# Second expert layer of a mixture block: hidden values computed transposed, from weights copied per tile

## What is computed

```python
shared = jax.nn.silu(xf @ Sg) * (xf @ Su) @ Sd
probs = jax.nn.softmax(xf @ Wr, axis=-1)
topk_p, topk_i = jax.lax.top_k(probs, K)
cw = jnp.zeros((T, n_exp), x.dtype).at[jnp.arange(T)[:, None], topk_i].add(topk_p)
def step(acc, ew):
    wg, wu, wd, c = ew
    y = jax.nn.silu(xf @ wg) * (xf @ wu) @ wd
    return (acc + y * c[:, None], None)
```

## Time and profile before

| | |
|---|---|
| median of 3 runs | 1652.86 us (1652.83 to 1653.16) |
| profiled execution: its own time | 1644.97 us |
| profiled execution: span, mean granted TensorE clock | 1643.2 us, 0.956 |
| busy in the span: TensorE passes, weight loads | 1487.4 us (91%), 1114.3 us (68%) |
| busy: VectorE, ScalarE, GpSimd | 1018.6 us (62%), 736.6 us (45%), 572.3 us (35%) |
| second expert stage, first transpose of x to last scatter | from 1444.9 us to 1584.4 us of the span |

### The profile page before, as it was taken

The page is one execution under the profiler, slowest core; times in us unless marked ns, Lnnn a source line. Parts: engine busy times, 40 slices in busy tenths (PEclk is TensorE's granted clock), DMA queues, the critical chain, the costliest instruction groups (busy, mean ns, idle before and its releaser), DMA issues. The chain is left out here.

```text
span 1643.2 us, 31228 instructions
## 1 busy us (share of the span) xinstructions
PE 1487.4 (91%) x9905; PEld 1114.3 (68%) x9905; DVE 1018.6 (62%) x3468; ACT 736.6 (45%) x1544; POOL 572.3 (35%) x994
## 2 busy tenths in 40 slices
PE   5999999983999999699799999999999597589987
PEld 3776676772999999565566666666666386468876
DVE  3345555453444444499898888888886286645558
ACT  3444444430222222345177777777777242244420
POOL 4123333344222222245532332322333165635530
PEclk9999999986999999899899999999999798889999
DMA  7001111115777777668857666667761575745556
GB/s 234 1 26 36 49 46 52 39 58 157 212 212 213 212 212 212 211 229 259 203 75 98 98 90 90 92 89 98 98 89 40 143 240 187 171 129 156 161 159 220
DMA packets 150592, 221.74 MB, mean 135 GB/s; under 512 B 23648, under 2 KB 98144, under 8 KB 150304
## 3 DMA queue, kind: packets, MB, share of 16 engines
q1 hardware_dynamic: 127904, 170.58, 45.2%
q0 software_dynamic: 13344, 36.55, 6.4%
q10 hardware_dynamic: 9184, 12.61, 2.5%
HBM read 141.16 MB, written 78.25 MB: 134 GB/s over the span
## 5 line engine op out<-in xcount | busy, mean ns | idle before, releaser
L2095 ACT ACTIVATE t_probs<-t_ps_st 128x512 f32<-128x512 f32 x576 | 313.2, 597 | 124.9 <-PE t_ps_st L2147 122.4
L2073 DVE CUSTOM_DVE_ANT_0 whole_sum<-t_ps_s,t_later 128x512 bf16<-128x512 f32 (+3 forms) x512 | 285.5, 586 | 14.0 <-PE t_ps_s L2133 11.9
L2049 POOL TENSOR_SCALAR_AFFINE_SELECT t_probs<-t_probs 128x128 f32<-128x128 f32 x512 | 137.4, 300 | 330.5 <-ACT t_probs L2095 328.9
L2133 PE MATMUL t_ps_s<-t_ks,t_qs 96*128 96x512 f32 (+3 forms) x768 | 247.8, 362 | 0.5 <-ACT t_neg_max L2085 0.5
L2147 PE MATMUL t_ps_st<-t_qs,t_ks 128*128 128x512 f32 (+3 forms) x768 | 242.7, 365 | 0.8 <-ACT t_probs L2095 0.8
L2147 PEld LDWEIGHTS t_ps_st<-t_qs,t_ks 128*128 128x128 f32 x768 | 136.8, 189 | 73.6 <-ACT t_probs L2095 40.2
L2073 DVE CUSTOM_DVE_ANT_0 whole_sum<-t_ps_s,t_later,t_first_max 128x512 bf16<-128x512 f32 (+3 forms) x256 | 140.5, 549 | 47.8 <-PE t_ps_s L2133 47.8
L2162 PE MATMUL t_ps_o<-t_probs,t_vs 128*17 128x256 f32 (+1 forms) x2560 | 154.9, 361 | 0.5 <-ACT whole_sum L2102 0.5
L2133 PEld LDWEIGHTS t_ps_s<-t_ks,t_qs 96*128 96x128 f32 x768 | 138.7, 190 | 18.0 <-DVE t_first_max L2073 1.6
L1460 POOL DMA_INDIRECT outputs_dram<-m_y,m_place x71 | 68.1, 959 | 208.8 <-DVE m_place L1535 201.1
L1490 PE MATMUL m_ps_h<-m_xt,m_w_t 128*128 128x128 f32 x1136 | 140.7, 278 | 0.0
(11 more groups left out here) (340 smaller groups left out, 2652.1 us busy)
## 6 DMA issues: line engine op xcount, KB each, us to landing
m_w_t<-in_w_dram SPq DMA_DIRECT2D x71, 512.0 KB, 4.4
t_qs<-qkt_dram SPq DMA_DIRECT2D x128, 128.0 KB, 5.6
t_ks<-qkt_dram SPq DMA_DIRECT2D x128, 128.0 KB, 5.7
m_x_t<-gathered_dram SPq DMA_DIRECT2D x79, 128.5 KB, 2.1
m_x_t<-gathered_dram SPq DMA_DIRECT2D x71, 129.0 KB, 2.1
d_ye<-outputs_dram SPq DMA_DIRECT2D x8, 1024.0 KB, 8.2
qkt_dram<-d_hi ACTq DMA_DIRECT2D x32, 256.0 KB, 5.2
qkt_dram<-d_lo SPq DMA_DIRECT2D x32, 256.0 KB, 7.2
```

The source lines that it names most:

```text
L2049: nc.gpsimd.affine_select(out=diag, in_=diag, compare_op=ALU.is_ge, fill=0.0, base=0, pattern=[[1, P]], channel_multiplier=-1).then_inc(ma ...
L2073: nc.vector.tensor_tensor_reduce(out=seen[:, (NP * p + x) % (RS + 1), 0:keys], in0=bank_of(p, x)[:, 0:keys], in1=masks, scale=1.0, scalar= ...
L2095: nc.scalar.activation(probs[:, p % 2, i // NST, base:base + STC], ps_st[(NX * p + i) % RT][:], ACT.Exp, scale=HD ** -0.5).then_inc(exp_re ...
L2133: nc.tensor.matmul(bank_of(p, x)[:, 0:keys], q[0:MAX_ROW, head, qc * P:(qc + 1) * P], k[0:MAX_ROW, head, k0:k0 + keys], start=True, stop=T ...
```

## The change

`run_experts` is removed and `run_gated_experts` takes its place for the second expert stage. ScalarE copies the gate and up weights of a tile's expert (128 partitions x 512 elements) from `wgu_sb` to a ring of three (`m_w_t`), two tiles ahead. The first layer takes them as stationary operand in blocks of 128 and streams x^T of 128 columns: four float32 products in place of two, and `m_ps_h` has hidden channels on its partitions. The products of the gate are therefore h^T already, so `turn_h`, `m_ps_ht` and its copy are gone, and VectorE writes `m_ht` itself. The loop is a turn shorter, the second layer stands two tiles behind the transposes of x in place of three, `m_ps_x` has two buffers, and ScalarE looks up experts too. SyncE's and GpSimd's programs are unchanged.

```diff
-def run_experts(nc, sb, pb, sem, c, name, E, gathered, outputs, kept, up, down, weights, late, by_row=False):
...
+def run_gated_experts(nc, sb, pb, sem, c, E, gathered, outputs, kept, w_up, w_down, weights, late):
+    ident = c["ident"]
+    n_list = 2 * NT + E - 1
+    F1 = P
+    tiles = kept["tiles"]
+    x_t = sb("m1_x_t", [P, RING, DM + 1])
+    w_t = sb("m1_w_t", [P, 3, KD, 2 * F1])
+    xt = sb("m1_xt", [P, 2, KD, P])
+    sig = sb("m1_sig", [P, 2, P])
+    act_g = sb("m1_act_g", [P, 2, P])
+    ht = sb("m1_ht", [P, 2, P])
+    y = sb("m1_y", [P, RING, DM])
+    place, spare = sb("m1_place", [P, n_list], U32), sb("m1_spare", [P, n_list])
+    ps_x = [pb(f"m1_ps_x{s}", [P, 2 * DM]) for s in range(2)]
+    ps_h = [pb(f"m1_ps_h{s}", [P, 4, P]) for s in range(2)]
+    ps_y = [pb(f"m1_ps_y{s}", [P, 2 * DM]) for s in range(2)]
+    x_loaded = [sem(f"m1_x_loaded{s}") for s in range(RING)]
+    stored = [sem(f"m1_stored{s}") for s in range(RING)]
+    place_taken, spare_ready, w_ready = sem("m1_place_taken"), sem("m1_spare_ready"), sem("m1_w_ready")
+    xt_done, xt_ready, h_done, sig_ready, gated, h_ready, y_done, y_ready = (sem("m1_" + n) for n in (
+        "xt_done", "xt_ready", "h_done", "sig_ready", "gated", "h_ready", "y_done", "y_ready"))
+
...
+    with nc.Block(no_gpsimd_drain=True) as block:
...
+        @block.tensor
+        def _(pe):
+            expert = {}
+
...
+            def turn_x(t):
+                pe.wait_ge(x_loaded[t % RING], 16 * (t // RING) + 16)
+                wait(pe, xt_ready, t - 1)
+                for j in range(KD):
+                    last = nc.tensor.transpose(ps_x[t % 2][:, j * P:(j + 1) * P], x_t[:, t % RING, j * P:(j + 1) * P], ident[:])
+                last.then_inc(xt_done, 1)
+
+            def go_up(t):
+                pe.wait_ge(w_ready, t + 1)
+                pe.wait_ge(xt_ready, t + 1)
+                wait(pe, h_ready, t - 1)
+                for f in range(2):
+                    for j in range(KD):
+                        last = nc.tensor.matmul(ps_h[t % 2][:, f, :], w_t[:, t % 3, j, f * F1:(f + 1) * F1], xt[:, t % 2, j, :],
+                                                start=(j == 0), stop=(j == KD - 1))
+                last.then_inc(h_done, 1)
+
+            def go_down(t):
+                pe.wait_ge(h_ready, t + 1)
+                wait(pe, y_ready, t - 1)
+                nc.tensor.matmul(ps_y[t % 2][:, 0:DM], ht[:, t % 2, :], w_down[:, 0, bass.ts(expert[t], DM)],
+                                 start=True, stop=True).then_inc(y_done, 1)
+
+            look_up(0)
+            pe.wait_ge(*weights)
+            for i in range(n_list + 2):
+                if live(i):
+                    turn_x(i)
+                if live(i - 1):
+                    go_up(i - 1)
+                if i % 4 == 3 and live(i + 1):
+                    look_up(i + 1)
+                if live(i - 2):
+                    go_down(i - 2)
+
+        @block.vector
+        def _(dve):
+            def gate(t):
+                dve.wait_ge(sig_ready, t + 1)
+                nc.vector.tensor_tensor(act_g[:, t % 2, :], ps_h[t % 2][:, 0, :], sig[:, t % 2, :], ALU.mult).then_inc(gated, 1)
+                dve.wait_ge(gated, t + 1)
+                wait(dve, y_done, t - 1)
+                nc.vector.tensor_tensor(ht[:, t % 2, :], ps_h[t % 2][:, 1, :], act_g[:, t % 2, :], ALU.mult).then_inc(h_ready, 1)
+
+            def finish(t):
+                dve.wait_ge(y_done, t + 1)
+                wait(dve, stored[t % RING], 16 * (t // RING))
+                nc.vector.tensor_copy(y[:, t % RING, :], ps_y[t % 2][:, 0:DM]).then_inc(y_ready, 1)
+
...
+            dve.wait_ge(spare_ready, 1)
+            for i in range(n_list + 2):
+                late(dve, i)
+                if live(i - 1):
+                    take_place(i - 1)
+                    gate(i - 1)
+                if live(i - 2):
+                    finish(i - 2)
+
+        @block.scalar
+        def _(act):
+            expert = {}
+
+            def take_weights(t):
+                if t % 4 == 0:
+                    expert.update(enumerate(entries(act, t, 0, E - 1), t))
+                wait(act, h_done, t - 2)
+                nc.scalar.activation(w_t[:, t % 3], w_up[:, :, bass.ts(expert[t], 2 * F1)], ACT.Copy).then_inc(w_ready, 1)
+
+            def copy_x(t):
+                act.wait_ge(xt_done, t + 1)
+                wait(act, h_done, t - 1)
+                nc.scalar.activation(xt[:, t % 2].rearrange("p k t -> p (k t)"), ps_x[t % 2][:, 0:DM], ACT.Copy).then_inc(xt_ready, 1)
+
+            def sigmoid(t):
+                act.wait_ge(h_done, t + 1)
+                wait(act, gated, t - 1)
+                nc.scalar.activation(sig[:, t % 2, :], ps_h[t % 2][:, 0, :], ACT.Sigmoid).then_inc(sig_ready, 1)
+
+            act.wait_ge(*weights)
+            take_weights(0)
+            take_weights(1)
+            for i in range(n_list + 1):
+                if live(i):
+                    copy_x(i)
+                if live(i - 1):
+                    sigmoid(i - 1)
+                if live(i + 2):
+                    take_weights(i + 2)
@@ -2857,8 +2823,8 @@
               lambda eng: load_shared(eng, shared, sg, su, sd),
               lambda eng: load_moe1_down(eng, moe1_loaded, wd_sb, w_d),
               lambda eng: load_moe1_up(eng, moe1_loaded, wgu_sb, w_gu))
-        phase(run_experts, c, "m1_", E1, gathered[1], outputs[1], kept, (2 * F1, wgu_sb, None), (F1 // P, wd_sb, None),
-              (moe1_loaded, 16 * (KD + 1)), lambda dve, i: weights_of_choice(dve, nc, kept, i), by_row=True)
+        phase(run_gated_experts, c, E1, gathered[1], outputs[1], kept, wgu_sb, wd_sb,
+              (moe1_loaded, 16 * (KD + 1)), lambda dve, i: weights_of_choice(dve, nc, kept, i))
         phase(finish, c, outputs[1], kept, total, xnt_all, shared, flat(out))
```

More of the change, by code:

```diff
@@ L1562, in _, with entries, live, load @@
                     relu_h(i - 1)
+def run_gated_experts(nc, sb, pb, sem, c, E, gathered, outputs, kept, w_up, w_down, weights, late):
[19 more added lines that the diff above has]
+        "xt_done", "xt_ready", "h_done", "sig_ready", "gated", "h_ready", "y_done", "y_ready"))
+    def entries(eng, t, what, top):
+        n = min(4, n_list - t)
+        return nc.values_load_multi_w_load_instructions(
+            tiles[0:1, what, t:t + n], engines=[eng.engine], min_val=0, max_val=top,
+            skip_runtime_bounds_check_because="every entry of the list is a minimum with this bound, or made from one")[1]
+    def live(t):
+        return 0 <= t < n_list
+    with nc.Block(no_gpsimd_drain=True) as block:
+        @block.sync
+        def _(sp):
+            row = {}
+            def load(t):
+                if t % 4 == 0:
+                    row.update(enumerate(entries(sp, t, 1, E * CAP + (E - 1) * P), t))
+                wait(sp, xt_done, t - RING + 1)
+                wait(sp, place_taken, t - RING + 1)
+                sp.dma_start(x_t[:, t % RING, :], gathered[bass.ds(row[t], P), :]).then_inc(x_loaded[t % RING], 16)
+            for t in range(n_list):
+                load(t)
+        @block.gpsimd
+        def _(pool):
+            def send(t):
+                pool.wait_ge(place_taken, t + 1)
+                pool.wait_ge(y_ready, t + 1)
+                nc.gpsimd.indirect_dma_start(out=outputs[:, :], out_offset=bass.IndirectOffsetOnAxis(ap=place[:, t:t + 1], axis=0),
+                                             in_=y[:, t % RING, :], in_offset=None).then_inc(stored[t % RING], 16)
+            nc.gpsimd.iota(spare[:], pattern=[[P, n_list]], base=2 * TOK, channel_multiplier=1,
+                           allow_small_or_imprecise_dtypes=True).then_inc(spare_ready, 1)
+            for t in range(n_list):
+                send(t)
+            for s in range(RING):
+                pool.wait_ge(stored[s], 16 * len(range(s, n_list, RING)))
+        @block.tensor
+        def _(pe):
+            expert = {}
+            def look_up(t):
+                expert.update(enumerate(entries(pe, t, 0, E - 1), t))
+            def turn_x(t):
[41 more added lines that the diff above has]
+                nc.vector.tensor_copy(y[:, t % RING, :], ps_y[t % 2][:, 0:DM]).then_inc(y_ready, 1)
+            def take_place(t):
+                dve.wait_ge(x_loaded[t % RING], 16 * (t // RING) + 16)
+                nc.vector.tensor_tensor(place[:, t:t + 1], x_t[:, t % RING, DM:DM + 1], spare[:, t:t + 1], ALU.min).then_inc(place_taken, 1)
+            dve.wait_ge(spare_ready, 1)
[10 more added lines that the diff above has]
+            def take_weights(t):
+                if t % 4 == 0:
+                    expert.update(enumerate(entries(act, t, 0, E - 1), t))
[19 more added lines that the diff above has]
+                    take_weights(i + 2)
```

169 lines of the change are left out of this document (removed).

## The result

The changed kernel took 1663.69 us (median of 15 runs, 1656.27 to 1669.28), beside 1654.59 us for the kernel before on the same chip (15 runs, 1650.61 to 1660.06): a ratio of 1.0052, 95% interval 1.0041 to 1.0063. The prediction was 1641.7 us, faster. It is 9.1 us slower instead.

What follows compares the result with a forecast made beforehand. TensorE was taken to set the pace in the second expert stage, busy 20.00 of 20 us. Terms -8.7 + 2.0 - 3.6 - 1.6 + 0.7 = -11.2 us gave a median of 1641.7 us, range 1637.5 to 1648.

Steps and rivals of the forecast that it cites:

- Transpose of h removed: On TensorE in the second expert stage: 79 tiles each save 0.11 us, 8.7 us in all.
- first layer in 8 passes: TensorE's first layer with weights stationary: 0.895 us a tile against 0.87, costing 2.0 us over 79 tiles.
- look-up on TensorE hidden: Expert look-ups move behind the previous tile's first layer: 19 of 20 give back 0.19 us each, 3.6 us.
- the rule of the Trainium skill: TensorE weight loads overlap passes in flight only for other row groups; the 8 loads would stand open, making the change slower.
- End of the stage: After the last tile, the second layer is released directly and the last scatter comes earlier: gain 1.6 us, bounds 0 and 1.6.
- ScalarE's look-ups: Every fourth tile ScalarE's own look-up overruns the period by 0.04 us: 0.7 us lost, bounds 0 and 6.6.
- The copies: New per-tile weight copies of 128x512 on ScalarE: about 0.63 us each, covered by TensorE's second layer and transposes.
- The sum: All terms of the second expert stage together: -11.2 us, giving a median of 1641.7 us.
- end of first layer to sigmoid 0.20: Hand-over from TensorE to ScalarE in the loop over two tiles, 0.20 us of its 3.03 us total.
- the cover is thin, 0.06 us: The loop over two tiles needs 3.03 us against TensorE's 3.09 at the new pace, leaving 0.06 us.
- The mark that the prediction gave for being wrong: In the profile after, TensorE waiting for m_h, because ScalarE is late, would show the forecast wrong.
- the fourth: Rival: ScalarE becomes the bound at 1.79 us a tile against 1.68, 7 us slower, 1660 us; chance 0.04.

Runs made afterwards that it cites:

- e3: Kernel before with its first layer streaming 256 columns in two halves of 128, doubling loads and passes there: 1649.98 us, ratio 1.0004 to the kernel before.
- e2: Changed kernel without ScalarE's weight copies and look-ups, first layer using expert 0's weights for every tile: 1636.36 us, ratio 0.9917 to the kernel before.
- g2: The changed kernel unaltered, run again on chip 14: 1636.70 us, ratio 0.9909 to the kernel before.
- g4: Changed kernel without ScalarE's weight copies and look-ups (fixed weights of expert 0), on chip 14: 1635.97 us, ratio 0.9909 to the kernel before.
- g3: The kernel before, nothing changed, run for its trace on chip 14: 1648.88 us, ratio 1.0 to the kernel before.
- f1: The changed kernel unaltered, run again on chip 0: 1663.80 us, ratio 1.003 to the kernel before.

## Why the prediction failed, point by point

On chip 14, where completions come on time, the terms can be read, some of them only together.

- **Transpose of h removed, first layer in 8 passes, look-up on TensorE hidden: right.** The period is an even 1.547 us (120.7 us over 78), forecast 1.545; passes stand 0.112 apart (0.89 for 8); no pause at look-ups. By the rule of the Trainium skill that the prediction drew on (TensorE: Matmul & The Clock Gate; it stands in the section The mechanism, not in the one named there) the loads would have stood in the open. The 8 loads of 0.192 us in 0.89 us disagree, and e3, which doubles them in the old kernel for 0.02 us a tile, disagrees too.
- **End of the stage: right.** From the start of the last first-layer pass to that of the last scatter it was 1579.4 to 1584.44, 5.1 us, and is 1573.3 to 1576.86, 3.6: 1.5 us saved, forecast 1.6. (The prediction's 1582.87 adds up to 1582.85.)
- **ScalarE's look-ups: 0.7 us forecast, nothing found.** Between change and e2's kind (no look-ups, no copies) on chip 14 (g2 and g4) the stage differs by less than 0.1 us. The copies take 0.625 us, forecast 0.63.
- **The sum: right there.** The stage's length fell from 139.08 us (g3, 1448.94 to 1588.02) to 127.14 (g2, 1449.71 to 1576.86), by 11.9 us with 11.2 forecast. The median time fell by 12.9, with four runs of the change.

**The step that failed** is "end of first layer to sigmoid 0.20" in the loop over two tiles, with its conclusion "the cover is thin, 0.06 us". I took one row's latency from TensorE to ScalarE as a constant and priced the thin cover only against ScalarE being busy. In the first comparison, and on chips 0 and 3, that latency was typically 0.8 to 1.1 us longer (at most 2.7) at about every third tile, with ScalarE idle. Cover was 0.17 us there rather than 0.06, and all beyond it, 0.95 of 1.12 us, went to the path. The cover was mis-sized too, on the safe side: sigmoid to gate took 0.31 us rather than 0.41, product to weight load 0.43 rather than 0.35. The mark that the prediction gave for being wrong, TensorE waiting for the product, did appear; the reason it gave for that, ScalarE late with its own work, did not.

**The account closes.** On the chips of the second kind the stage of the change is longer by 139.3 to 144.4 less 120.7, 19 to 24 us. The phases ahead of it are longer too: the first tile's last first-layer pass comes at 1452.3 us in the mean of the fourteen traces of the first kind and at 1459.7 in the six of the second, 7.4 later.

Nearly all of that arises in one phase, `back`: the same pass of TensorE comes 0.5 us later at the end of attention (1284 us) and 7.5 later at 1431. `back` scatters by index, loses records, and has late completions of its own: from 1310 to 1431 us the six traces hold 46 to 52 records of four of TensorE's hand-overs there, 11 to 18 of them 0.75 us or more behind the pass, up to 4.6; the fourteen hold 60 to 62 and none above 0.65. No instruction of `back` was changed, so the lateness doesn't belong to the new loop.

For the change that makes 1636.7 + 7.4 + 20 (f1's 140.4 less 120.7) = 1664, measured 1663.7 and 1663.8. For the kernel before, 1649.7 (the mean of its four medians on chips of the first kind) + 7.4 = 1657.1 already, and it measured 1654.6, 1655.8 and 1658.0, so its own second expert stage can have lost little. That is an estimate which takes it that `back` costs the kernel before the same 7.4 us: no trace of it on such a chip was taken. By this estimate the change meets a loss of some 20 us that the kernel before doesn't, and gives back its 12.9.

**What stays open:** why completions are late on some chips; whether the recording of the trace, whose updates are missing there, takes part in it (every run on record comes with a span and a granted clock, so none is known to have gone without recording); what the late completions of `back` have in common with those of the last expert stage; and whether the kernel before escapes because it has 18 loads and passes in 1.63 us instead of 24 in 1.55, or because its longer loop over three tiles covers them. A high mean rate by itself, rival C, isn't what it takes: from 1320 to 1380 us `back` has 505 loads and passes in 60 us, 8.4 per us, and late completions, while the first expert stage has 13.9 per us (52 in 3.73 us, TensorE full), near the change's 15.5, and none on either kind of chip. What the last of the change's rate adds isn't known: e3, with 15.3 per us in a loop over three tiles, never met such a chip.

None of the prediction's rivals named late completions. Nearest in form was the fourth, with ScalarE's chain as the bound and 1660 us: the same chain, made long by a wait instead of work.

No run points to a version that beats both kernels on both kinds of chip. The change is the faster by 0.9% on one kind and the slower by 0.3 to 0.5% on the other.

## What to carry over

When a change takes a tile of slack out of a loop across engines, price the loop with each hand-over between engines late, not only with each engine busy: here 0.17 us of cover met a hand-over 1.1 us late. A comparison on one chip can have the sign of that chip; before explaining a difference, run the unaltered change again beside the variant that seems to mend it, since a fourth buffer looked like a cure of 26 us, and beside the unaltered change on chip 14 it did nothing. Count records in the traces before comparing them: a difference there separated the two kinds of chip more sharply than the times of the kernel before did.

## What the runs showed of the hardware that was not expected

- The completion of a TensorE pass reached ScalarE 0.31 us after the pass's start in most tiles, and 1.4 us (at most 2.8) after it in about every third, in the same program on the same chip, with TensorE itself on time. TensorE's other hand-overs were recorded late there too, those of ScalarE and VectorE not.
- The change had this on chip 0 (45 tiles of 79) and not on 14, the change without copies on chip 3 (46 tiles) and not on 1 and 14. In `back`, which is the same in all kernels, hand-overs of TensorE were recorded up to 4.6 us after the pass in the six traces of the second kind, and no later than 0.65 us in the fourteen of the first.
- In the first expert stage, where 16 of a tile's 26 passes have the same form, VectorE followed the last of them after 0.42 us on both kinds of chip (0.57 at most); so the form alone does not bring it about.
- A look-up of four numbers from SBUF cost ScalarE's sequencer 0.31 us and TensorE's 0.33, and neither was seen in the period of the change. In the kernel before, TensorE's was: 1.83 us instead of 1.63 in every fourth tile.
